# A new order of all engines for a two-layer gated mixture-of-experts block: the third batch's shared down products behind the experts, routing and puts batch by batch, the memsets of unused rows first

## The chip, the cores and the metric

One core of one Trainium2 chip. The metric is the device time of one run of the whole kernel in microseconds (us), given as the median of several runs.

## The reference

Input x has 4 batches of 256 tokens with 256 channels. Two layers are computed one after the other, `x = x + ffn(cond(x))`. The conditioning (bi_wkv) of both layers scans each channel over time forwards and backwards; k = v = the side input:

```python
ek = exp(min(k, 30)); ekv = ek * v
a = a * decay + ekv_t; b = b * decay + ek_t        # over t, forwards and backwards
num = nf + nb - ekv + exp(min(u + k, 30)) * v
den = df + db - ek + exp(min(u + k, 30))
out = sigmoid(r) * (num / max(den, 1e-8)) * (0.8 + 0.2 * tf)
```

Layer 0's ffn is a routed mixture with a shared part. Each token goes to its top 2 of 8 experts (capacity 320 rows each, places given out in the order of the tokens), each expert is `silu(gate) * up` of width 176 and a down product, weighted by a softmax of two logits. The shared part is the same with width 704 for every token. Layer 1's ffn is `relu(x @ W_up.T) @ W_down.T + sum(softmax(top 2 logits)) * (x @ W_expert)`.

## The kernel before

Engines are called PE (matrix products), DVE (vector), ACT (activations), POOL (GpSimd) and SP (DMA issue). Everything is held in SBUF; each engine runs one instruction stream written out in order, and semaphores tie the streams together. Tables of numbers at the head of the file say behind which "chunk" each engine does which piece of work.

A chunk is one hidden product. The shared part has 6 chunks per batch (5 of 128 hidden columns and one of 64), an expert has 2. The list `chunks` holds first the shared chunks of batches 0 to 2 and `SPLIT` chunks of batch 3 (together `nearly` = 20), then 16 of the experts (20 to 35), then the rest of batch 3. For a chunk PE makes the up and gate products (`shared_up`, `expert_up`; `hb` and at first `dn` are its PSUM banks), ACT takes the silu into `gate_a` (`silu`), DVE multiplies (`hidden`, into `hid` or `hidm`). PE may write a bank again only when the hidden product of the chunk that last used it is done (`chunk_before`). `shared_down(b)` is the down product of batch b's shared part, 12 matmuls into `dn`; `take_shared(b)` on DVE adds it to xt. `idle_products` are matmuls without use, `FILL` says how many stand ahead of which chunk.

The conditioning of a batch is cut in 6 steps (`wkv`): step 0 the forward scans of df, step 1 those of nf (and a cap of ek), step 2 and 3 the backward scans of df and nf (and a cap of euk), step 4 a reciprocal, step 5 the scaling of it. POOL does the products and sums between (`values`, `bonus`, `denominator`, `numerator`, `gate_num`, `hidden0`); for the batches in `H0_ON_VECTOR` DVE does the product h0 that ends them (`xc<-euv,rden`), for layer 1 those in `Q1_ON_VECTOR` the product `euk<-euv,rden`. `STEPS0` and `STEPS1` say how many steps of layer 0 and of layer 1 stand ahead of the hidden product of each chunk; ACT's scalings (`scale_fwd`) follow the same plan. `HOLD` names the numerators that POOL holds until DVE's step 4 has read.

Routing goes in rounds over batches (`ROUNDS`). `turn_rows(b)` on PE turns h0 to rows of tokens and makes the logits, ahead of the chunks in `TURN_AT`; ACT copies them (`turned`); `route(r)` on DVE picks the experts ahead of the hidden product in `ROUTE_AT`; `ranks(r)` on PE counts places behind the chunk in `RANK_AT`; `place(r)` on DVE makes `put_at` behind the hidden product in `PLACE_AT`. POOL then puts token rows with indirect DMAs (`scatter`, two for each of 8 tiles of tokens) into `slots_in` in DRAM; `SPREAD` says how many tiles have been put by which place of its stream. When all have landed SP loads them in pairs of experts (`load_pair`), PE turns them (`slots_T`, `tp<-ident,buf`), and they are split in two parts (`bufT`), as the experts' weights are (`mup_w`).

The experts' outputs go to `slots_out` in DRAM. Behind them POOL gathers them for each batch (`gather`), DVE adds them up to x1 (`combine`), PE turns x1 (`turn_x1`, `tp<-ident,xt`) and makes layer 1's products. Gathers start when the last expert's output is written and POOL has done what stands ahead of them, a numerator of layer 1 among it (`numerator`). The last batch's shared down product is split: its first tile stands ahead of `turn_x1(0)`, the second behind it.

Six memsets (`pads`) zero the unused rows of hid, sdn_s, hidm and mdn_s.

## Time and profile before

| | us |
|---|---|
| median of 3 runs (lowest, highest) | 180.54 (179.97, 181.22) |
| the profiled execution, span from first to last instruction | 168.4 |
| busy: PE, DVE, POOL, ACT | 151.0, 129.0, 102.4, 82.7 |

The profile records the profiled execution from its first to its last instruction; what lies ahead of it and behind it is in the run's time only. Its times count from the start of the span. Busy times overlap between engines, so their sum says nothing; what matters is which engine the chain of waits goes through. "xN" behind a PE row of a chain counts weight loads and matmuls together.

### The profile page before, as it was taken

What the parts mean: (1) busy time and instruction counts of PE and PEld (TensorE: products, weight loads), DVE (VectorE), ACT (ScalarE), POOL (GpSimd) and SP (SyncE); (2) the same over time, 40 slices, a digit from 0 to 9 for tenths busy, and PEclk for the clock granted to TensorE, in tenths of its full rate; (3) what the DMA queues carried; (4) which work ended last, traced back from release to release, by engine and by line L of the source; (5) the groups of instructions that cost most, each with busy time, mean ns of one, the idle gap of its engine ahead of it and who ended that gap; (6) DMA issues with size and microseconds to landing.
All of it is one profiled execution on the core that took longest, in us unless ns stands there. A gap on an engine that the chain in (4) does not pass through costs nothing.

```text
span 168.4 us, 2521 instructions
## 1 busy us (share of the span) xinstructions
PE 151.0 (90%) x790; PEld 133.2 (79%) x790; DVE 129.0 (77%) x290; ACT 82.7 (49%) x189; POOL 102.4 (61%) x109
## 2 busy tenths in 40 slices
PE   0398999999999999967999999999999929989991
PEld 0277888988898898854999999999988718879890
DVE  1899999979995987916467897899787845498634
ACT  3799951792372082103277853982734101336750
POOL 5376569796489877895049456637715777750330
PEclk9999999999999999995599999999999987999999
DMA  4789999996012132169402072022222333332211
GB/s 121 230 327 373 390 406 347 228 275 234 25 62 66 45 111 91 56 188 352 138 4 80 0 225 91 2 78 78 78 79 81 90 97 93 108 103 71 66 62 62
DMA packets 14844, 23.63 MB, mean 140 GB/s; under 512 B 1974, under 2 KB 10375, under 8 KB 14704
## 3 DMA queue, kind: packets, MB, share of 16 engines
q1 hardware_dynamic: 13152, 19.48, 35.8%
q0 software_dynamic: 1536, 3.99, 7.5%
q8 instruction: 6, 0.10, 0.3%
q14 instruction: 6, 0.05, 0.1%
q10 hardware_dynamic: 144, 0.00, 0.0%
HBM read 15.29 MB, written 8.39 MB: 141 GB/s over the span
## 4 chain that ended last, share of the span: by engine, by line
PE 72%; DVE 11%; DMA 6%; issue 5%; POOL 2%; ACT 2%; SPq 0%; DVEq 0%; POOLq 0%; ACTq 0%
PE hb L1057 31%; PE dn L1057 23%; PE tp L1057 5%; PE hb L1074 3%; PE tp L1178 3%; DMA buf<-slots_in 2%; PE dn L1074 2%; DMA wu_s<-wu 2%; POOL buf L512 2%; PE tp L1096 2%; DMA slots_in<-htok,put_at 1%; PE dk L1057 1%; DVE nf L777 1%; DVE xt L994 1%; DVE rden L859 1%
## 5 line engine op out<-in xcount | busy, mean ns | idle before, releaser
L1057 PE MATMUL hb<-xc,sup_s 128*128 128x256 f32 x136 | 30.8, 381 | 0.0
L1057 PEld LDWEIGHTS hb<-xc,sup_s 128*128 128x128 f32 x136 | 25.4, 190 | 3.2
L1057 PE MATMUL hb<-bufT,mup_w 128*112 128x320 f32 (+1 forms) x144 | 25.7, 336 | 0.7 <-issue 0.7
L619 ACT ACTIVATE gate_a<-hb 128x256 f32<-128x256 f32 (+3 forms) x38 | 15.1, 401 | 20.8 <-PE hb L1057 20.1
L1057 PEld LDWEIGHTS hb<-bufT,mup_w 128*112 128x112 f32 (+1 forms) x144 | 23.6, 195 | 1.5 <-issue 1.1
L1057 PE MATMUL dn<-sdn_s,hid 128*128 128x256 f32 x96 | 22.8, 394 | 0.1
L1057 PE MATMUL dn<-mdn_s,hidm 112*128 112x256 f32 x96 | 22.1, 380 | 0.0
L1057 PEld LDWEIGHTS dn<-sdn_s,hid 128*128 128x128 f32 x96 | 19.0, 200 | 3.2 <-DVE hid L887 0.5
L1057 PEld LDWEIGHTS dn<-mdn_s,hidm 112*128 112x128 f32 x96 | 17.7, 190 | 2.4 <-issue 0.3
L449 POOL TENSOR_TENSOR mup_w<-mup_s,mup_w 128x704 fp32r<-128x704 f32 x8 | 13.5, 1694 | 8.6 <-ACT mup_w L634 8.6
L422 POOL DMA_INDIRECT slots_in<-htok,put_at x16 | 15.9, 991 | 4.6 <-issue 4.3
L573 ACT ACTIVATE gd<-df,gain 128x255 f32<-128x255 f32 x16 | 8.1, 507 | 19.9 <-DVE df L770 19.5
L396 POOL TENSOR_TENSOR euk<-euk,df 128x512 f32<-128x512 f32 x7 | 8.9, 1278 | 7.8 <-DVE df L777 7.5
L403 POOL TENSOR_TENSOR euv<-euv,nf 128x512 f32<-128x512 f32 x7 | 9.0, 1279 | 7.3 <-DVE dk L819 4.9
L821 DVE RECIPROCAL dk<-dk 128x256 f32<-128x256 f32 x7 | 12.4, 1766 | 0.2
L887 DVE TENSOR_TENSOR hidm<-hb,gate_a 112x320 f32<-112x320 f32 (+1 forms) x16 | 7.6, 484 | 5.7 <-ACT gate_a L619 5.5
L1057 PE MATMUL dn<-k,ident 128*128 128x256 f32 x14 | 5.6, 585 | 7.0 <-DVE df L770 7.0
L380 POOL TENSOR_TENSOR euv<-euk,k 128x512 f32<-128x512 f32 x8 | 10.3, 1291 | 1.0 <-DVE euk L792 1.0
L777 DVE TENSOR_TENSOR_SCAN nf<-dk,nf,gn 128x255 f32<-128x255 f32 x14 | 9.6, 728 | 1.5 <-ACT gn L573 1.5
L1057 PEld LDWEIGHTS dn<-k,ident 128*128 128x128 f32 x14 | 4.2, 312 | 7.9 <-issue 6.9
L887 DVE TENSOR_TENSOR hid<-hb,gate_a 128x256 f32<-128x256 f32 (+1 forms) x22 | 9.1, 415 | 1.8 <-ACT gate_a L619 1.6
L895 DVE TENSOR_TENSOR bufT<-tp,bufT 128x512 fp32r<-128x512 f32 (+1 forms) x12 | 6.8, 594 | 4.7 <-ACT bufT L628 4.7
(146 smaller groups left out, 304.6 us busy)
## 6 DMA issues: line engine op xcount, KB each, us to landing
mup_s<-mup SPq DMA_DIRECT2D x4, 704.0 KB, 14.5
slots_in<-outb SPq DMA_DIRECT2D x10, 256.0 KB, 9.3
slots_out<-outb SPq DMA_DIRECT2D x8, 256.0 KB, 2.2
buf<-slots_in SPq DMA_DIRECT2D x4, 384.0 KB, 4.8
k<-k_cm SPq DMA_DIRECT2D x4, 256.0 KB, 4.8
xc<-x_cm SPq DMA_DIRECT2D x4, 256.0 KB, 8.0
sup_s<-sup SPq DMA_DIRECT2D x2, 512.0 KB, 8.7
xt<-x_tm SPq DMA_DIRECT2D x1, 1024.0 KB, 10.8
```

The source lines that it names most:

```text
L380: nc.gpsimd.tensor_tensor(euv[:, n % 2], euk[:, l, b], k[:, b], ALU.mult).then_inc(euv_ready, 1)
L396: nc.gpsimd.tensor_tensor(euk[:, l, b], euk[:, l, b], df[:], ALU.add).then_inc(den_summed, 1)
L403: nc.gpsimd.tensor_tensor(euv[:, n % 2], euv[:, n % 2], nf[:], ALU.add).then_inc(num_ready[n], 1)
L422: nc.gpsimd.indirect_dma_start(out=slots_in, out_offset=bass.IndirectOffsetOnAxis(ap=put_at[:, j, n:n + 1], axis=0), in_=htok[:, n], in_of ...
L449: nc.gpsimd.tensor_tensor(mup_w[:, e % 2, 1], mup_s[:, e], mup_w[:, e % 2, 0].bitcast(F32), ALU.subtract).then_inc(mup_low, 1)
L573: nc.scalar.activation(dst[:, c, 0:T - 1], fwd[:, c, 0:T - 1], ACT.Copy, scale=gain[:, l, b, c:c + 1]).then_inc(scaled, 1)
L619: nc.scalar.activation(dst, src, ACT.Silu).then_inc(silu_ready, 1)
L777: nc.vector.tensor_tensor_scan(rev(both[:, c, 0:T - 1]), d, rev(gained[:, c, 0:T - 1]), both[:, c, T - 1:T], ALU.mult, ALU.add).then_inc(b ...
L821: after(tick(nc.vector.reciprocal(pair, pair)))
L887: nc.vector.tensor_tensor(dst, up, g, ALU.mult).then_inc(hid_ready, 1)
L1057: return nc.tensor.matmul(dst, w, m, start=first, stop=last)
L1074: last = nc.tensor.matmul(ub[u][:, half * T:half * T + T], sup_s[:, at:at + P], xc[:, 0, c], start=c == 0 and half == 0, stop=c == CH - 1, ...
```

## The change

The first round of routing no longer takes two batches: there are four rounds, one for each batch. `SPLIT` is 4, so four chunks of batch 3 stand ahead of the experts (`nearly` = 22, experts 22 to 37) and two behind; `shared_down` has places ahead of the experts only for batches 0 and 1, and batch 2's stands behind the experts and behind the last shared chunks. The pads are zeroed ahead of `values(0)`. h0 of batch 2 moves from POOL to DVE, layer 1's q1 of batch 2 from DVE to POOL. All places of steps, routing, turns and fills are new. In all 12 idle products stand ahead of the shared chunks (12 and 7 before).

```diff
-ROUNDS = ((0, 2), (2, 3), (3, 4))
+ROUNDS = ((0, 1), (1, 2), (2, 3), (3, 4))
-SPLIT = 2
+SPLIT = 4
-FILL = {2: 5, 3: 7, 6: 7}
+FILL = {5: 9, 3: 2, 4: 1}
-HOLD = (1, 6)
+HOLD = (5,)
-TURN_AT = (6, 11, 15)
-ROUTE_AT = (6, 11, 15)
-RANK_AT = (7, 13, 16)
-PLACE_AT = (8, 12, 15)
+TURN_AT = (8, 13, 16)
+ROUTE_AT = (2, 8, 13, 16)
+RANK_AT = (5, 9, 15, 18)
+PLACE_AT = (5, 10, 14, 17)
...
-STEPS0 = (6, 1, 2, 0, 0, 0, 0, 0, 2, 4, 1, 0, 2, 0, 0, 0, 0, 0, 0)
+STEPS0 = (4, 2, 0, 0, 0, 2, 2, 0, 1, 1, 1, 1, 1, 1, 2, 0, 0, 0, 0, 0, 0, 0, 0, 0)
...
-DOWN_BEHIND = (10, 14, 19)
-TAKE_BEHIND = (15, 16, 19)
-GATE_AT = (6, 7)
-SPREAD = {5: 0, 8: 0, 10: 2, 11: 8, 13: 8, 14: 8, 15: 8}
-H0_ON_VECTOR = (0, 3)
-Q1_ON_VECTOR = (2, 3)
-PADS_AT = (5, 5, 5, 5, 5, 5)
+DOWN_BEHIND = (7, 15)
+TAKE_BEHIND = (11, 14)
+GATE_AT = (4, 7)
+SPREAD = {1: 2, 10: 4, 15: 8}
+H0_ON_VECTOR = (0, 2, 3)
+Q1_ON_VECTOR = (3,)
...
+            pool.wait_ge(consts, 7 + E)
+            for i, pad in enumerate(pads):
+                nc.gpsimd.memset(pad, 0.0).then_inc(padded, 1)
+                pool.wait_ge(padded, i + 1)
             values(0)
...
-                    pads_behind(4 * b + 1)
...
             halves()
+            for b in range(len(DOWN_BEHIND), B - 1):
+                take_shared(b)
             combine(0)
...
+                if b >= 1 and j == 0:
+                    pe.wait_ge(h0_ready[b], 1)
...
-                if b == B - 1:
+                if b == len(DOWN_BEHIND):
                     pe.wait_ge(mo_taken, 2 * E)
...
-                    pe.wait_ge(sh_taken, B - 1)
+                    pe.wait_ge(sh_taken, len(DOWN_BEHIND))
...
             for u in range(nlate, nchunks):
                 shared_up(u)
+            for b in range(len(DOWN_BEHIND), B - 1):
+                shared_down(b)
             shared_down(B - 1, range(TB - 1))
```

What stands in a row on POOL around the puts, before (`slots_in<-htok,put_at` is a put, `xc<-euv,rden` the product h0, `euv<-euk,k` the bonus, the three lines behind the first puts are denominator, numerator and gate of batch 3):

```order
L396 TENSOR_TENSOR euk<-euk,df 128x512
L403 TENSOR_TENSOR euv<-euv,nf 128x512
L408 TENSOR_TENSOR euv<-euv,xc 128x512
L413 TENSOR_TENSOR xc<-euv,rden 128x512
L380 TENSOR_TENSOR euv<-euk,k 128x512
L422 DMA slots_in<-htok,put_at 2560x256 x4
L396 TENSOR_TENSOR euk<-euk,df 128x512
L403 TENSOR_TENSOR euv<-euv,nf 128x512
L408 TENSOR_TENSOR euv<-euv,xc 128x512
L422 DMA slots_in<-htok,put_at 2560x256 x12
```

and now:

```order
L395 TENSOR_TENSOR euk<-euk,df 128x512
L402 TENSOR_TENSOR euv<-euv,nf 128x512
L407 TENSOR_TENSOR euv<-euv,xc 128x512
L379 TENSOR_TENSOR euv<-euk,k 128x512
L421 DMA slots_in<-htok,put_at 2560x256 x8
L395 TENSOR_TENSOR euk<-euk,df 128x512
L402 TENSOR_TENSOR euv<-euv,nf 128x512
L407 TENSOR_TENSOR euv<-euv,xc 128x512
L421 DMA slots_in<-htok,put_at 2560x256 x8
```

Batch 2's h0 has left the row, and eight puts (batches 0 and 1) stand ahead of batch 3's sums instead of four.

On DVE around experts 4 and 5, before (`hidm` 112x320 and 64x320 are the two hidden products of an expert, `bufT<-tp,bufT` the split of turned rows, `nf<-dk,nf,gn` the backward scan, the cap is `euk<-euk,dk`, step 4 are the three rows with `dk<-`):

```order
L887 TENSOR_TENSOR hidm<-hb,gate_a 64x320
L895 TENSOR_TENSOR bufT<-tp,bufT 128x2x256 x2
L887 TENSOR_TENSOR hidm<-hb,gate_a 112x320
L777 SCALAR_TENSOR_TENSOR nf<-dk,nf,gn 128x255 x2
L784 TENSOR_TENSOR euk<-euk,dk 128x512
L887 TENSOR_TENSOR hidm<-hb,gate_a 64x320
L895 TENSOR_TENSOR bufT<-tp,bufT 128x2x128
L818 TENSOR_TENSOR dk<-euk,dk 128x256
L819 SCALAR_TENSOR_TENSOR dk<-euk,dk 128x256
L821 RECIPROCAL dk<-dk 128x256
```

and now:

```order
L883 TENSOR_TENSOR hidm<-hb,gate_a 64x320
L891 TENSOR_TENSOR bufT<-tp,bufT 128x2x256 x2
L773 SCALAR_TENSOR_TENSOR nf<-dk,nf,gn 128x255 x2
L780 TENSOR_TENSOR euk<-euk,dk 128x512
L814 TENSOR_TENSOR dk<-euk,dk 128x256
L815 SCALAR_TENSOR_TENSOR dk<-euk,dk 128x256
L817 RECIPROCAL dk<-dk 128x256
L883 TENSOR_TENSOR hidm<-hb,gate_a 112x320
L883 TENSOR_TENSOR hidm<-hb,gate_a 64x320
```

The backward scan, the cap and all of step 4 have moved ahead of the first hidden product of expert 5.

On PE from the last experts' down products (`dn<-mdn_s,hidm`) to the second part of the last batch's down product, before:

```order
L1057 MATMUL dn<-mdn_s,hidm 128x256 x12
L1057 MATMUL hb<-xc,sup_s 128x256 x14
L1057 MATMUL dn<-sdn_s,hid 128x256 x6
L1238 MATMUL tp<-ident,xt 128x128 x4
L1057 MATMUL dn<-sdn_s,hid 128x256 x6
```

and now:

```order
L1055 MATMUL dn<-mdn_s,hidm 128x256 x12
L1055 MATMUL hb<-xc,sup_s 128x256 x6
L1055 MATMUL dn<-sdn_s,hid 128x256 x18
L1240 MATMUL tp<-ident,xt 128x128 x4
L1055 MATMUL dn<-sdn_s,hid 128x256 x6
```

Eight up products have gone ahead of the experts, and twelve down products have come.

## Rows read from the trace of the kernel before

**Rows 1.** The page, part 4: shares of the chain that ended last.

```profile
PE 72%; DVE 11%; DMA 6%; issue 5%; POOL 2%; ACT 2%; SPq 0%; DVEq 0%; POOLq 0%; ACTq 0%
```

**Rows 2.** Windows: busy us (and count) of each engine during the experts.

```profile
core 0: us, PE busy (x) PEld busy (x) DVE busy (x) ACT busy (x) POOL busy (x), PEclk, DMA share, GB/s
79.00:121.00 42.00, 42.00 (x247) 39.99 (x247) 34.44 (x56) 25.65 (x52) 22.62 (x16) 0.95 0.27 85
```

**Rows 3.** The chain in order of time (start, us, what), last put to first expert.

```profile
70.08 2.30 DMA slots_in<-htok,put_at
...
72.82 3.51 DMA buf<-slots_in
...
78.75 4.98 PE hb L1057 x18
```

**Rows 4.** Timeline, first values and the pads (start, us, engine line operation).

```profile
6.18 1.26 POOL L368 TENSOR_TENSOR ekv<-ek,k 128x512 f32<-128x512 f32 x1 [3.02 <-DVE ek L788]
...
7.90 1.26 DVE L770 TENSOR_TENSOR_SCAN nf<-dk,ekv 128x256 f32<-128x256 f32 x2
...
32.85 0.52 POOL L444 MEMSET hid<- 64x512 f32 x1
...
36.45 0.47 POOL L444 MEMSET hidm<- 64x128 f32 x2
```

**Rows 5.** Timeline of DVE: steps 0, 4 and the end of step 5.

```profile
18.31 1.27 DVE L770 TENSOR_TENSOR_SCAN df<-dk,ek 128x256 f32<-128x256 f32 x2
...
24.39 0.42 DVE L818 TENSOR_TENSOR dk<-euk,dk 128x256 f32<-128x256 f32 x1
...
27.72 0.42 DVE L887 TENSOR_TENSOR hid<-hb,gate_a 128x256 f32<-128x256 f32 x1
```

**Rows 6.** Timeline of DVE: one round of route, h0, and one round of place.

```profile
50.17 0.23 DVE L914 MAX8 top<-lg 128x8 f32<-128x8 f32 x2
...
51.16 0.41 DVE L887 TENSOR_TENSOR hid<-hb,gate_a 64x256 f32<-64x256 f32 x1
...
56.71 0.69 DVE L832 TENSOR_TENSOR xc<-euv,rden 128x512 f32<-128x512 f32 x1
...
57.78 0.18 DVE L932 TENSOR_TENSOR ohp<-tp,oh 128x32 f32<-128x32 f32 x1
...
58.57 1.27 DVE L770 TENSOR_TENSOR_SCAN df<-dk,ek 128x256 f32<-128x256 f32 x2
```

**Rows 7.** The chain in order of time: one batch's down products.

```profile
42.19 5.18 PE dn L1057 x24
```

**Rows 8.** The page, part 5: the puts (busy, mean ns, idle before).

```profile
L422 POOL DMA_INDIRECT slots_in<-htok,put_at x16 | 15.9, 991 | 4.6 <-issue 4.3
```

**Rows 9.** Line 837 (ns: shortest, median, longest): products of layer 1 on DVE.

```profile
L837 DVE TENSOR_TENSOR euk<-euv,rden x2: 692/1108/1524, 117.8 to 133.0; 128x512 f32<-128x512 f32 x2
```

**Rows 10.** Timeline of DVE around experts 4 and 5.

```profile
109.00 1.29 DVE L895 TENSOR_TENSOR bufT<-tp,bufT 128x512 fp32r<-128x512 f32 x2 [0.66 <-ACT bufT L628]
110.56 0.49 DVE L887 TENSOR_TENSOR hidm<-hb,gate_a 112x320 f32<-112x320 f32 x1 [0.27 <-ACT gate_a L619]
```

**Rows 11.** The chain in order of time: expert 6, last experts, last batch's down products.

```profile
113.12 2.63 PE hb L1057 x18
...
120.96 5.40 PE dn L1057 x24
...
139.40 3.68 PE dn L1057 x12
```

**Rows 12.** Timeline behind the experts: first gather, first transposes, second batch's sums.

```profile
130.08 1.02 POOL L512 DMA_INDIRECT buf<-slots_out,get_at  x1
...
138.31 1.09 PE L1238 MATMUL tp<-ident,xt 128*128 128x128 f32 x4 [3.00 <-DVE xt L999]
...
141.69 0.88 DVE L994 SCALAR_TENSOR_TENSOR xt<-buf,cw,xt 128x256 f32<-128x256 f32 x2 [0.85 <-DMA buf<-slots_out,get_at]
```

**Rows 13.** Windows: busy us and granted clock behind the first transposes of x1.

```profile
138.00:140.00 2.00, 1.69 (x6) 1.54 (x7) 0.56 (x2) 0.56 (x1) 1.57 (x2) 0.51 0.46 131
```

More of the change, by code:

```diff
@@ L31 @@
 L1X = CH * (2 * C + E)
-SPLIT = 2
+SPLIT = 4
 EARLY_AT = 1
 EARLY = 7
-FILL = {2: 5, 3: 7, 6: 7}
+FILL = {5: 9, 3: 2, 4: 1}
 AHEAD = 5
-HIGH_AT = (3, 10)
-HOLD = (1, 6)
-SILU_FIRST = (0, 1, 2, 3, 5, 7, 8, 13, 14, 16, 17, 18)
-TURN_AT = (6, 11, 15)
-ROUTE_AT = (6, 11, 15)
-RANK_AT = (7, 13, 16)
-PLACE_AT = (8, 12, 15)
-LOW_AT = (7, 8)
-FETCH_AT = 35
-STEPS = 6
-STEPS0 = (6, 1, 2, 0, 0, 0, 0, 0, 2, 4, 1, 0, 2, 0, 0, 0, 0, 0, 0)
-STEPS1 = (0, 0, 0, 0, 0, 0, 0, 0, 0, 0, 0, 0, 0, 1, 0, 1, 0, 0, 0, 2, 1, 0, 0, 0, 3, 2, 0, 2, 0, 3, 0, 1, 1, 0, 2, 0, 3, 1, 0, 1, 0, 0, 0, 0)
-DOWN_BEHIND = (10, 14, 19)
-TAKE_BEHIND = (15, 16, 19)
-GATE_AT = (6, 7)
-SPREAD = {5: 0, 8: 0, 10: 2, 11: 8, 13: 8, 14: 8, 15: 8}
-H0_ON_VECTOR = (0, 3)
-Q1_ON_VECTOR = (2, 3)
-PADS_AT = (5, 5, 5, 5, 5, 5)
+HIGH_AT = (4, 18)
+HOLD = (5,)
+SILU_FIRST = (0, 2, 5, 6, 7, 9, 10, 11, 13, 15, 17, 18, 20)
+TURN_AT = (8, 13, 16)
+ROUTE_AT = (2, 8, 13, 16)
+RANK_AT = (5, 9, 15, 18)
+PLACE_AT = (5, 10, 14, 17)
+LOW_AT = (8, 8)
+FETCH_AT = 33
+STEPS = 6
+STEPS0 = (4, 2, 0, 0, 0, 2, 2, 0, 1, 1, 1, 1, 1, 1, 2, 0, 0, 0, 0, 0, 0, 0, 0, 0)
+STEPS1 = (0, 0, 0, 0, 0, 0, 0, 0, 0, 0, 0, 0, 0, 0, 0, 0, 0, 1, 2, 0, 0, 1, 1, 0, 0, 1, 2, 2, 1, 0, 4, 0, 2, 0, 1, 3, 1, 0, 1, 1, 0, 0, 0, 0)
+DOWN_BEHIND = (7, 15)
[4 more added lines that the diff above has]
+Q1_ON_VECTOR = (3,)
 def adaln_ffn(nc, x_cm, x_tm, k_cm, cond, wu, router, sup, sdn, mup, mdn, l1w, out):
@@ L439, in _ @@
             pads = (hid[JR:P, :, JC], sdn_s[JR:P, JC], hidm[IB:IA, :, 1], mdn_s[IB:IA, :, 1], hidm[0:IB, :, 1, CAP:], hidm[:, :, 0, CAP:])
-            def pads_behind(step):
-                for i, pad in enumerate(pads):
-                    if PADS_AT[i] == step:
-                        nc.gpsimd.memset(pad, 0.0).then_inc(padded, 1)
-                        pool.wait_ge(padded, i + 1)
             def low_mup(e):
```

## The prediction

> **What bounds the kernel now.** I read the chain that ended last, then the windows, then each engine in order of time. In the chain [rows 1] TensorE (PE) has 72% of the span, VectorE (DVE) 11%, DMA 6%. During the experts PE is never idle: 42.00 us busy in the 42 us from 79 to 121 [rows 2]. PE stops in only two places. Before the experts it waits for the puts (the indirect DMAs that write token rows into slots_in): the last starts at 70.08 and lands after 2.30, and the loads that follow take until 76.33 [rows 3]; PE had been through its shared products 2.6 us before that, with two short idle times. Behind the experts it waits for the first gathers: they start at 130.08 and the transposes of x1 at 138.31, with PE idle for 3.0 us before these [rows 12]. So what counts is when the last put starts, whether PE stays fed between 79 and 126.4 (end of the experts), and what happens until 138.3.
>
> The profiled execution is known by its span, 168.4; the median of the runs is 180.54. I take the 12.14 between them as what lies around a span and leave it fixed.
>
> **Pads first.** The six memsets run from 32.85 to 36.45 + 0.47 = 36.92, 4.07 us [rows 4]. Ahead of the first batch they begin when the constants end (3.16), so end near 7.3. The product ekv then ends at 7.3 + 0.05 + 1.26 = 8.6, where it ended at 7.44. The scan of nf that needs it began at 7.90 [rows 4] and will begin at 8.65: +0.75 us on DVE and on the start of PE. That is certain within 0.25.
>
> **Routing batch by batch, from there to the last put.** I walk DVE's queue of the new order, in order, with measured pitches. Steps 0 to 3 with both caps took 18.31 to 24.39, 6.08; steps 4 and 5 took 24.39 to 27.72, 3.33 [rows 5]; of these a pair of scans is 1.16 to 1.30, a cap 0.58, step 5 0.61 and so step 4 2.72. Routing of two tiles took 50.17 to 51.16, 0.99; placing them 57.78 to 58.57, 0.79; a hidden product is 0.35; h0 on DVE is 0.69 and a wait, 0.84 more than step 5 alone [rows 6]. On PE twelve products take 5.18, so 0.432 each [rows 7].
> - DVE starts the second batch at 18.31 + 0.75 = 19.07. Steps 0 to 3, hid, steps 4 and 5, hid: 29.2. Routing of batch 0: 30.2. Three hids with ACT's tanh between: 31.4. Steps 0 and 1 of batch 2, cap, hid: 34.6. Place 0: 35.4. Steps 2, 3, cap, two hids, step 4: 42.0. Route 1: 43.0. hid, step 5 with h0, hid, step 0, hid, place 1: 47.5.
> - POOL, freed of the pads and of h0 of batch 2, has the values of batch 3 done by about 42.1 and puts batch 0 from there; a put costs 0.991 and (4.6 / 16) 0.29 of idle time, 1.28 [rows 8]. Batch 1's four follow at 47.5 and end at 52.6. Three products of 1.3 end at 56.7.
> - DVE from 47.5: step 1, hid, taking batch 0's sums (0.6), step 2, hid, step 3, cap, route 2, hid, steps 4 and 5 with h0, hid, place 2: 59.8. Only then may batch 2's puts start, so POOL waits 3 us. Four puts end at 64.9.
> - PE at 59.5 is through batch 1's down products; the turn of batch 3 waits for place 2 (59.8); 0.93 for the turn, ten products at 0.432 (4.3) and 0.35 for the ranks: 65.4. Place 3 ends at 66.2. The last four puts start at 66.25 to 70.1.
>
> So the last put starts at 70.1 against 70.08: 0.0. The chain is no longer POOL's issue but DVE's queue and PE's ranks. An uncertainty of 1 us each way is what 14 hids of 0.33 or 0.42 and the ACT waits make; if DVE's queue ran free of them POOL could start batch 2's puts at 56.7, and the last put 4.3 earlier at 65.8.
>
> One of the new terms is h0 of batch 2 on DVE. Its row beside POOL's puts is 0.69 [rows 6]; but the same kind of product, L837, took 1.524 beside a POOL product and 0.692 a second time [rows 9]. The Trainium skill (GPSIMD Engine Reference, section 1, Specifications) says that POOL shares its SBUF interfaces with VectorE and that they contend where a DVE instruction has two inputs in SBUF; the 1.52 agrees. In the new order POOL issues puts at that moment, so I take 0.69; by the page's rule with a product beside it, place 1 and all behind it would be 0.83 later.
>
> **PE's cut.** Seven idle products go, 12 down products move behind the experts and 8 up products come ahead of them: (7 + 12 - 8) x 0.432 = 4.75 us less PE ahead of the experts, all of it work beside the puts' chain. PE would be done at about 70.8 instead of 73.8 and be idle for 4.5 us until the first transposes. Since the last put sets these, this is worth nothing.
> It touches the clock, though. After the two idle times before the experts the first expert's 18 products took 4.98 [rows 3] where a later expert's take 2.63 [rows 11]: PE at the lower of its two levels for most of it, 2.35 lost. I take the same loss and 0.2 more for the longer idle time, between -0.6 and +1.1.
>
> **Experts.** The change puts 18 steps of the second layer among the 16 expert chunks, where 15 stood, and takes one product of 1.52 (L837) off DVE. PE needs the hidden product of a chunk before it may write its bank again, one expert later. The tight place is chunk 32, the first of expert 5: two steps now stand ahead of its hidden product, the scan of nf with its cap and step 4: 1.27 + 0.58 + 2.72 = 4.57. In the trace DVE was free of bufT at 109.00 + 1.29 and did the hidden product of expert 5 at 110.56, after 0.27 of waiting for ACT [rows 10]. By the new order I find DVE free at 109.55 (the hidden products of expert 4 are done 0.8 earlier, and bufT follows ACT), so the hidden product ends at 109.55 + 4.57 + 0.45 = 114.55. PE reached expert 6 at 113.12 [rows 11]. PE stalls for 1.45. At chunk 28 (step 4 ahead of it) hid ends at 101.5 where PE wants it at 101.6: 0. At chunk 35 (three steps ahead) 121.6 against 121.55: 0.05. Sum +1.5; bounds 0 (DVE early by 1.5) and +3.0 (late by 0.5 at each of the three). So the experts end at 127.9 instead of 120.96 + 5.40 = 126.36 [rows 11].
>
> **Tail.** The gathers waited for nf's numerator of the last batch on POOL, which now stands among the experts. What is left is expert 7's store: issued 0.8 after the products end, landing 2.0 later. The first gather starts 3.0 behind the experts' end where it started 3.72 behind (130.08 [rows 12] - 126.36): -0.7. PE behind the experts: 6 + 12 + 6 products, 10.4 us, against 20 products, 8.6; the transposes come 11.25 behind, so PE's idle time shrinks from 3.0 to 0.9. The moved 5.18 us is thus half hidden in what was idle, at no cost to the end.
> After the 3.0 idle the clock was granted at 0.51, the lower level, from 138 to 140 [rows 13]; six down products took 3.68 [rows 11] where they take 2.59, and the four transposes about 0.6 too much: 1.7 lost. With 0.9 of idle I expect the full clock. Of this only part reaches the end: batch 1's gathers already end the wait of DVE at 141.69 [rows 12], and they begin 0.8 later (+1.5 - 0.7). Its x1 is then ready at 144.25, its transposes end at 144.75 against 145.1, ACT's tanh starts at 144.8 instead of 145.49. So -0.7 from there on, where the experts' end was +1.5: the tail gives back 2.2.
>
> **Sum.** 0.0 + 0.2 + 1.5 - 2.2 = -0.5: a span of 167.9, and 180.0.
>
> **Rivals.**
> 1. Experts starved (slower). If DVE comes to chunk 32 later by 0.5 or more, the stall is 2 us and likely draws the clock down, as the idle time of 3.0 did [rows 13]; a low stretch cost 1.7 to 2.35, 2.1 in the middle. Then 180.0 + 0.5 + 2.1 = 182.6. For it: PE has no slack there [rows 2] and 4.57 us stand in one row. Against: ACT's waits may be shorter. It decides from a stall of some 2 us. Chance 0.23.
> 2. No stall: DVE is 1.5 earlier at chunk 32. Then 180.0 - 1.5 = 178.5. For it: DVE waited for ACT twice, 0.66 and 0.27, just ahead of this place [rows 10]. Chance 0.14.
> 3. Puts earlier. If place 2 is early enough that POOL never waits, the last put is up to 4.3 earlier, and PE, busy until 70.8, lets that through nearly whole; 2.5 as the middle: 177.5. Against: two DVE rounds are added to the queue and the pads cost 0.75. Chance 0.13.
>
> My forecast, in which puts, stall and tail nearly cancel, has 0.50.
>
> Below 1% a measurement of this kernel can hardly be told from no change. Faster by over 1% (under 178.7) are rivals 2 and 3: 0.27. Slower by over 1% (above 182.35) is rival 1: 0.23. The likeliest case alone spans 178.8 to 182.0; the range reaches to the middle of rival 3 and past rival 1: 177.4 to 183.0.
>
> **What would show it.** Right: POOL idle ahead of the ninth put, and the last put near 70; ekv ending at 8.6; PE idle for over 4 us before the experts; a stall of 1 to 2 us ahead of expert 6's products, released by hidm; the first gather 3 us behind the last expert product; a clock of 1.00 behind the transposes of x1. Wrong: no wait on hidm within the experts (rival 2), the last put before 68 (rival 3), a low clock among the experts (rival 1).

## The result, and the profile after

The changed kernel takes 187.96 us (median of 4 runs, 186.38 to 188.83) where the kernel before, run beside it, takes 180.88 (4 runs, 179.97 to 182.33): a ratio of 1.039, with the interval 1.030 to 1.047. It is slower by 7 us where 180.0 was forecast, outside the range. Here and below a ratio and its interval compare only the fast runs of the two kernels (some executions show a slower state), so they need not be the quotient of the medians beside them.

The profiled execution of the changed kernel has a span of 184.6 us and its own time is 186.38, so 1.8 us lie around a span, and not 12.14. The execution of before whose rows stand above (span 168.4) was some 10 us shorter than the runs beside which it stood. Why is told with the experiments; one of them gave a second trace of before, with a span of 179.0.

The chain that ended last, by engine [rows 1 before]:

```profile
span 184.6 us, 2510 instructions
...
PE 42%; DVE 29%; DMA 8%; issue 7%; another core or an unknown queue 6%; POOL 3%; ACT 2%; DVEq 0%; SPq 0%; POOLq 0%; ACTq 0%
```

PE had 72% of this chain and DVE 11%; now PE has 42% and DVE 29%. The chain now runs through DVE's queue for much of the time ahead of the experts. The part from the last put to the first expert, in order of time [rows 3 before]:

```profile
76.68 2.30 DMA slots_in<-htok,put_at
...
79.00 2.77 DMA buf<-slots_in
...
85.50 4.05 PE hb L1055 x18
```

The last put starts at 76.68 instead of 70.08, the first expert at 85.50 instead of 78.75. From the put on nothing has changed: 8.82 us between these two where there were 8.67. So the loss lies ahead of the last put. POOL's timeline shows what the puts wait for, and [rows 8] have their line of the page:

```profile
65.39 1.01 POOL L421 DMA_INDIRECT slots_in<-htok,put_at  x1 [6.44 <-DVE put_at L934]
...
72.85 0.97 POOL L421 DMA_INDIRECT slots_in<-htok,put_at  x1 [2.62 <-DVE put_at L934]
```

```profile
L421 POOL DMA_INDIRECT slots_in<-htok,put_at x16 | 15.8, 988 | 13.9 <-DVE put_at L934 9.1
```

A put is as cheap as it was (988 ns), but POOL stands idle for 6.44 us ahead of the ninth and for 2.62 ahead of the thirteenth, until DVE's put_at is written. So why is DVE late? The end of its third routing, in its timeline (a whole round took 0.99 us in [rows 6]):

```profile
55.48 0.16 DVE L913 FIND_INDEX8 idx<-top,lg 128x8 uint32<-128x8 f32 x1
55.56 2.08 DVE L914 TENSOR_TENSOR dtop<-top 128x2 f32<-128x2 f32 x1
57.56 0.18 DVE L918 TENSOR_TENSOR oh<-idx,iota_e 128x32 f32<-128x32 uint32 x1
57.77 1.21 DVE L919 TENSOR_TENSOR hot<-oh 128x16 bf16<-128x16 f32 x1
```

and POOL at the same time:

```profile
55.10 1.29 POOL L395 TENSOR_TENSOR euk<-euk,df 128x512 f32<-128x512 f32 x1
56.33 1.28 POOL L402 TENSOR_TENSOR euv<-euv,nf 128x512 f32<-128x512 f32 x1
57.68 1.26 POOL L407 TENSOR_TENSOR euv<-euv,xc 128x512 f32<-128x512 f32 x1
```

dtop subtracts two columns from two and takes 0.14 us in all three rounds of before. Here it lasts 2.08 us, and it ends at 57.64, when POOL's second product ends (57.61). hot, 0.17 otherwise, lasts 1.21 and ends at 58.98, when the third product ends (58.94). The first routing has the same (0.63 and 1.12), and slot of the first place (0.69 for 0.16). Behind it PE waits, since the counts of the round need hot, and its queue is in order:

```profile
59.03 0.18 PE L1055 MATMUL tp<-hot,before 128*128 128x16 bf16 x1 [3.03 <-DVE hot L919]
```

The tail, first in the chain [rows 11, 12 before], then as a window in which the seventh number is the granted clock [rows 13 before]:

```profile
127.53 5.39 PE dn L1055 x24
...
133.74 4.11 DMA slots_out<-outb
...
138.73 1.01 POOL buf L508
...
146.90 1.10 PE tp L1240 x4
...
148.61 11.39 another core or an unknown queue
...
160.09 0.70 ACT hid L709
```

```profile
146.00:153.00 7.00, 6.10 (x17) 5.01 (x18) 3.63 (x9) 0.60 (x1) 5.18 (x6) 0.51 0.33 94
```

The first gather starts 5.8 us behind the end of the experts (132.92), since the last small store of expert 7 took 4.11 to land (137.85) and the gather starts 0.88 behind that. The clock behind the transposes of x1 is again at its lower level (0.51). And 11.4 us of the chain end in ScalarE (ACT), released by nothing that the profile shows; the same wait is in the kernel before on such a chip (9.1 us in before_again below), so it is not the change's.

### The profile page after: what moved, and what is told of

Read it like the earlier page. It is cut to its first block, busy times and chain, and to the rows that moved or that the text cites. A ratio compares the mean times of both kernels' runs of the same rounds, so it can differ in the third digit from the quotient of the medians.

```text
span 184.6 us, 2510 instructions
## 1 busy us (share of the span) xinstructions
PE 153.5 (83%) x778; PEld 132.6 (72%) x778; DVE 134.4 (73%) x298; ACT 82.3 (45%) x190; POOL 102.0 (55%) x109
## 4 chain that ended last, share of the span: by engine, by line
PE 42%; DVE 29%; DMA 8%; issue 7%; another core or an unknown queue 6%; POOL 3%; ACT 2%; DVEq 0%; SPq 0%; POOLq 0%; ACTq 0%
PE hb L1055 19%; PE dn L1055 17%; DVE df L773 3%; DVE nf L766 3%; PE tp L1178 3%; DMA slots_out<-outb 2%; DVE df L766 2%; DVE nf L773 2%; DVE dk L817 2%; DVE hid L883 2%; DMA wu_s<-wu 2%; POOL buf L508 2%; DMA buf<-slots_in 1%; DMA buf<-slots_out,get_at 1%
## 5 line engine op out<-in xcount | busy, mean ns | idle before, releaser
L1055 PE MATMUL hb<-bufT,mup_w 128*112 128x320 f32 (+1 forms) x144 | 24.7, 327 | 0.7 <-issue 0.5
L1055 PEld LDWEIGHTS hb<-bufT,mup_w 128*112 128x112 f32 (+1 forms) x144 | 22.5, 188 | 2.2 <-POOL mup_w L442 1.0
L1055 PE MATMUL dn<-sdn_s,hid 128*128 128x256 f32 x96 | 24.0, 412 | 0.0
L1055 PEld LDWEIGHTS dn<-sdn_s,hid 128*128 128x128 f32 x96 | 19.8, 208 | 3.0
L508 POOL DMA_INDIRECT buf<-slots_out,get_at x8 | 7.6, 954 | 9.5 <-DMA slots_out<-outb 7.4
L1055 PE MATMUL dn<-htok,hid 128*128 128x256 f32 x32 | 9.5, 450 | 3.9 <-ACT hid L709 3.9
L395 POOL TENSOR_TENSOR euk<-euk,df 128x512 f32<-128x512 f32 x7 | 8.9, 1276 | 6.5 <-DVE df L773 6.3
L516 POOL TENSOR_TENSOR xt<-gate_a,xt 128x256 f32<-128x256 f32 x4 | 3.1, 797 | 16.7 <-ACT gate_a L728 16.7
L1178 PE MATMUL tp<-ident,buf 128*128 128x128 f32 x40 | 7.2, 313 | 5.2 <-DMA buf<-slots_in 4.9
L402 POOL TENSOR_TENSOR euv<-euv,nf 128x512 f32<-128x512 f32 x7 | 8.9, 1274 | 4.2 <-DVE dk L815 3.0
```

The costliest lines, as they stand in the source:

```text
L395: nc.gpsimd.tensor_tensor(euk[:, l, b], euk[:, l, b], df[:], ALU.add).then_inc(den_summed, 1)
L402: nc.gpsimd.tensor_tensor(euv[:, n % 2], euv[:, n % 2], nf[:], ALU.add).then_inc(num_ready[n], 1)
L508: nc.gpsimd.indirect_dma_start(out=got_of(b, j, i), out_offset=None, in_=slots_out, in_offset=bass.IndirectOffsetOnAxis(ap=get_at[:, j, b ...
L1055: return nc.tensor.matmul(dst, w, m, start=first, stop=last)
L1178: last = nc.tensor.transpose(tp[t % 2][:, at:at + P], buf[:, q % 2, 2 * i + k_, c * P:(c + 1) * P], ident[:])
```

## The experiments

Theory P: a small DVE operation lasts until the POOL product beside it ends, and the new order puts routings beside such products. Its rival, theory O: the order itself is late (four rounds for three, a batch's down products ahead of the last routing, counts two chunks behind it). The chips differ, as will be seen, so each time stands with that of before on the same chip.

### Parts of the change by themselves

The kernel before again, unchanged.

> The kernel before, unchanged, for a second trace. The first trace of it has a span of 168.4 where its runs take 180.9; the changed kernel's run of 186.4 has a span of 184.6, 1.8 around it. If 1.8 lies around every span, an ordinary execution of before has a span of about 179 and a stall of some 10 us that the first trace did not have: then ACT's wait behind the first x1 (5 us beyond its releaser in the changed kernel) should be seen here too. If instead 12 us lie around the span of before, this span is 168 to 170.

181.27 us. Its trace has a span of 179.0 where the one above had 168.4. The rows in which the two differ are ACT's; they follow below under the stall.

The fills first, alone, in the kernel before:

```diff
+            pool.wait_ge(consts, 7 + E)
+            for i, pad in enumerate(pads):
+                nc.gpsimd.memset(pad, 0.0).then_inc(padded, 1)
+                pool.wait_ge(padded, i + 1)
             values(0)
...
-                    pads_behind(4 * b + 1)
```

> Before, with the six memsets ahead of the first values and nothing else. Queue theory: the first ekv ends at 8.6 instead of 7.44, DVE starts batch 1 0.75 later, POOL has 4.1 us less around 33; the last put within 1 us of before, time +0 to +0.8 us. Port theory (a DVE instruction with two inputs in SBUF, or a plain scalar one, is held while POOL runs one): oscale and the first cap of ek take over 1.2 us each where they took 0.16 and 0.69, as in the changed kernel, but their wait lies inside the 0.75, so the same time: +0 to +0.8.

182.1, 0.8 above the same kernel without it. (Their ratios to before are 1.011, 1.004 to 1.018, and 1.009, 1.001 to 1.016, so by the time alone the two can't be told apart.) Every milestone ahead of the puts is 0.75 to 0.8 later (dtop of the first round 36.26 for 35.48, put_at 44.11 for 43.33). The term of +0.75 was right for these.

Batch 2's down products behind the experts, alone: the order of before with SPLIT 4, DOWN_BEHIND (10, 14), TAKE_BEHIND (15, 16), FETCH_AT 37, and the steps of layer 1 behind the two chunks more.

> Before's order with one part of the change: batch 2's shared down product behind the experts, two up chunks of batch 3 ahead of them (SPLIT 4), all tables of before otherwise, shifted by the two chunks. Queue theory: PE ends its work ahead of the experts 1.7 us earlier (idle there 3.1 instead of 1.4 us), the last put is where it was, PE's idle time behind the experts shrinks from 3.0 to about 1.3 us, and the time stays within 1 us. Rival (the cut of cover is what costs): more low clock at the first expert and batch 2's take on DVE late for the first x1, +2 us or more.

179.32, ratio 0.997 (0.991 to 1.003). This part costs nothing and gains nothing that can be told.

The fills back in their old place, but in the changed kernel:

```diff
-            pool.wait_ge(consts, 7 + E)
-            for i, pad in enumerate(pads):
-                nc.gpsimd.memset(pad, 0.0).then_inc(padded, 1)
-                pool.wait_ge(padded, i + 1)
             values(0)
...
                     pool.wait_ge(ekv_ready, b + 3)
+                    if b == 1:
+                        for i, pad in enumerate(pads):
+                            nc.gpsimd.memset(pad, 0.0).then_inc(padded, 1)
+                            pool.wait_ge(padded, i + 1)
```

> The changed kernel with the six fills of unused rows back behind the products of batch 1. Theory: the first values come 0.75 to 0.85 us earlier, but the fills then stand beside the first routing or behind it; everything up to the last put moves by no more than that, time 186.5 to 187.5 (0.5 to 1.3 less than the changed kernel's 187.96). Rival (the fills ahead hold the whole core back by more than their 0.8 us, since oscale and the cap of ek lasted 1.31 and 1.24 beside one of them): over 2 us less.

193.09, ratio 1.068 (1.059 to 1.078): neither theory, and 5 us worse than the changed kernel. PE's timeline says why:

```profile
41.08 8.11 PE L1055 MATMUL dn<-sdn_s,hid 128*128 128x256 f32 x24 [6.12 <-issue]
```

The first down products need the rows filled, and in the new order they stand behind chunk 7, not 10. With the fills ending at 40.98, PE stands for 6.12 us and then needs 8.11 for what takes 5.3, at a granted clock of 0.66 from 41.1 to 49.1. So the fills first cost 0.75 in the old order, and in the new one are what makes it possible at all. I had priced them only by the queue they stand in, not by who waits for them.

### POOL's products beside the routing

The numerator of batch 3 behind DVE's pair product, so that it and the gate product leave the third routing:

```diff
-HOLD = (5,)
+HOLD = (1, 3, 5)
```

> The changed kernel with HOLD (1, 3, 5) instead of (5,): POOL's numerators of batches 1 and 3 of layer 0 wait until DVE's step 4 has read, so no POOL product runs beside the routing of rounds 0 and 2. Port theory: dtop and hot of round 2 take 0.15 and 0.17 instead of 2.08 and 1.21, those of round 0 the same instead of 0.63 and 1.12; the place of round 2 comes 3 us or more earlier, the last put starts near 73 instead of 76.7, time -3 us against the changed kernel. Queue theory (DVE's instructions were merely waiting for something of their own): same lengths as in the changed kernel, and the numerators' wait makes it 0 to 1 us slower.

184.62, ratio 1.018 (1.008 to 1.027) where the changed kernel had 1.039: 3 us given back, 1.8 of them at the first expert (83.73). DVE's row beside the one product that stayed (L395, 55.27 to 56.55):

```profile
55.72 0.86 DVE L914 TENSOR_TENSOR dtop<-top 128x2 f32<-128x2 f32 x1
56.51 0.18 DVE L918 TENSOR_TENSOR oh<-idx,iota_e 128x32 f32<-128x32 uint32 x1
56.72 0.18 DVE L919 TENSOR_TENSOR hot<-oh 128x16 bf16<-128x16 f32 x1
```

dtop fell from 2.08 to 0.86 and hot from 1.21 to 0.18, when the products that had lain beside them went. The first routing kept its collisions (0.79 and 1.12): the expectation that they would go too failed, and the last put came at 74.83 where 73 was expected.

The same, and h0 of batch 1 moved to DVE, to free the first routing too (H0_ON_VECTOR (0, 1, 2, 3)).

> The changed kernel with HOLD (1, 3, 5) and H0_ON_VECTOR (0, 1, 2, 3): no product of POOL but one denominator stands beside a routing any more. Theory (the routing's small VectorE operations last until the POOL product beside them ends): in the first routing dtop takes 0.15 and hot 0.17 instead of 0.79 and 1.12, the h0 of batch 1 costs VectorE 0.69 more, so the first expert starts 0.5 to 1.0 us ahead of the 83.73 of the kernel with HOLD (1, 3, 5) alone, and the time is 183.5 to 184.5. Rival (the rounds batch by batch are late for another reason, and what the products cost there is covered): first expert within 0.3 us of 83.73, time as that kernel, 184.6 or above.

185.61, ratio 1.027 (1.018 to 1.035). The first routing is clean (0.14 and 0.17; in the third dtop still takes 0.87 beside the one denominator), and yet the first expert starts at 85.04, 1.3 later than in hold_num: the expectation failed. DVE and POOL:

```profile
29.25 1.67 DVE L828 TENSOR_TENSOR xc<-euv,rden 128x512 f32<-128x512 f32 x1 [0.34 <-POOL euv L407]
```

```profile
29.10 1.27 POOL L379 TENSOR_TENSOR euv<-euk,k 128x512 f32<-128x512 f32 x1
```

The moved product takes 1.67, for 0.69 otherwise: it now lies beside a POOL product itself. A collision was moved, not removed.

The other way round, in the kernel before: its first four puts taken away from beside the second routing, so that POOL's products stand there (the entry 10: 2 of SPREAD removed).

> The kernel before with one entry of SPREAD taken out ({13: 8, 14: 8, 15: 8}), so that POOL's products of batch 3 stand where the first four puts stood, beside the second routing. Theory (POOL's product holds the small operations): dtop of that routing, 0.14 now, lasts 0.5 to 2.1 us and hot, 0.17 now, 0.2 to 1.3; the sixteen puts in one row end at 73 to 75 and the time is 1 to 3 us above the kernel before. Rival (the long dtop and hot of the changed kernel come from something else in it, such as the form of one batch a round): both stay at 0.14 and 0.17.

181.54 beside 181.6; ratio 1.011 (1.003 to 1.018). dtop and hot kept their 0.14 and 0.17, as the rival said, but the operation between them did not:

```profile
50.69 0.14 DVE L918 TENSOR_TENSOR dtop<-top 128x2 f32<-128x2 f32 x1
50.81 1.25 DVE L922 TENSOR_TENSOR oh<-idx,iota_e 128x32 f32<-128x32 uint32 x1
```

POOL's gate product ran from 50.74 to 52.01; oh ends at 52.06. So it happens in the old order too, once a product lies there, and which of the small operations is caught depends on the moment. The last put came 2.1 later than in before_again, but the time did not follow.

H0 of batch 2 back on POOL (H0_ON_VECTOR (0, 3)).

> The changed kernel with h0 of batch 2 back on POOL (H0_ON_VECTOR (0, 3)). Theory: VectorE gives 0.69 up at 62.7 but POOL's product of 1.27 then stands there and ohp, slot or put_at of the third place last until it ends, so put_at(2) comes at 64.0 to 65.2 instead of 64.44, and the time is within 1 us of 187.96. Rival (the h0 on VectorE was one of the costs): 1 to 3 us less.

182.14 beside 170.35, ratio 1.055 (1.048 to 1.063). POOL waits 3.28 us for rden with h0 at the head of its queue, the puts begin at 50.05 and not at 44.30, put_at of the third place stands at 66.74 and not at 64.44, and the first expert starts at 89.93, where the unchanged kernel on such a chip has 86.12. So by the traces moving this h0 to DVE, which I had weighed as a cost of up to 0.83, is right in the new order. The times leave it open: the ratio to before is no worse than the 1.065 of after_again below (the intervals overlap), though the median is 2.7 us longer.

How much these products cost was measured by making them short, in kernels that leave that part of the computation out. First batch 1's h0 and batch 2's products (one of five edits):

```diff
-                nc.gpsimd.tensor_tensor(euk[:, l, b], euk[:, l, b], df[:], ALU.add).then_inc(den_summed, 1)
+                m = 8 if n == 2 else T
+                nc.gpsimd.tensor_tensor(euk[:, l, b, :, 0:m], euk[:, l, b, :, 0:m], df[:, :, 0:m], ALU.add).then_inc(den_summed, 1)
```

> The changed kernel with five of POOL's products cut to 8 of 256 columns: batch 1's h0, and batch 2's bonus, denominator, numerator and gate product, those beside the first and third routing. It leaves that part of the computation out. Theory: dtop and hot of both routings take 0.14 and 0.17, PE no longer waits 1.46 and 3.03 for hot, the third place ends near 60 and not 64.6, the last put starts at 71.5 to 73.5 and not 76.7, the first expert at 80.5 to 82.5 and not 85.5; 2 to 4 us of the 6.75 stay, by the new order. Rival (the order alone is at fault): the first expert still starts at 84 or later.

178.28 beside 170.38, ratio 1.065 (1.050 to 1.080), so the time shows no gain; the trace does. I had mistaken the batch: those beside the third routing are batch 3's, and it kept its 2.08 and 1.20. In the first routing dtop and hot are 0.48 and 0.94 shorter, 1.42 in all, and all of it arrives: first expert 84.72, for 86.12 in the unchanged kernel beside it. Then batch 3's too (n in (2, 3)):

> As after_short, but batch 3's denominator, numerator and gate product, those beside the third routing, are cut to 8 of 256 columns too. It leaves that part of the computation out. Theory: dtop and hot of the third routing take 0.14 and 0.17 instead of 2.08 and 1.21, PE's wait of 3.03 for hot goes, and the last put starts 2.5 to 3.2 us ahead of after_short's 75.91, at 72.7 to 73.4; the first expert starts at 81.5 to 82.3. So of 6.75 us some 4.4 are the products', some 2.5 the order's. Rival (the order alone): less than 1 us gained over after_short's 84.72.

173.65 beside 169.18, ratio 1.037 (1.017 to 1.056).

```profile
71.66 2.33 DMA slots_in<-htok,put_at
...
80.59 4.48 PE hb L1060 x18
```

dtop takes 0.14 and hot 0.17, PE's wait for hot is gone, the last put starts at 71.66 and the first expert at 80.59, earlier than expected. So of the 7.37 us by which the unchanged kernel was late on such a chip (86.12 - 78.75), 5.53 go with POOL's products and 1.84 stay with the order, 0.75 of it the fills and up to 0.53 the slot of the first place, which still lasts 0.69 for 0.16 beside a product. Of the 5.53, 4.38 are the four rows themselves (0.48 and 0.94, 1.93 and 1.03); the other 1.15 isn't parted by any run. Shorter products also shorten POOL's own queue, and the clock has a share: after the 3.03 us idle the 24 down products took 7.11 in after_again, at a granted clock of 0.76, and without the idle time 5.43. But the first trace of the changed kernel has the same idle time, then 5.3 for them at 1.00, and its first expert starts only 0.62 earlier (85.50), so the clock was worth some 0.6 there.

```profile
59.20 7.11 PE L1055 MATMUL dn<-sdn_s,hid 128*128 128x256 f32 x24
```

The last step of the order, counts one chunk closer to the routing (RANK_AT (5, 9, 15, 17)):

> The changed kernel with RANK_AT (5, 9, 15, 17): PE counts the last batch's tokens after 6, not 10, products of the row between. Theory (the last place waits 1.18 for these counts and VectorE's put_at ends at 72.07): put_at ends 1.0 to 2.2 us earlier, the last put starts at 74.5 to 75.7, and the time falls by 1 to 2 us against the changed kernel on the same kind of chip (179.4 beside 170.4, or 188.0 beside 180.9). Rival: PE waits for hot instead and nothing is gained.

179.02 beside 169.18, ratio 1.069 (1.051 to 1.087); nothing gained. PE's counts come 1.75 earlier (69.64 for 71.39 in after_again), put_at only 0.57, the last put at 76.70 for 77.27: ahead of the place DVE has a pair of scans and two hidden products of its own, and it had waited only 0.45 for the counts. The expected 1.0 to 2.2 was too much, read off a wait of 1.18 in another execution.

Which DVE operations are hit can be read from all twenty traces together with the kernel. In 53 cases a product or sum on DVE with both inputs in SBUF (dtop, oh, hot, slot, h0, q1, and one combine) started while a product of POOL was running. 52 of them were held until a product of POOL ended: the small ones ended with it, the long ones behind it (h0 and q1, 0.69 alone, 0.55 behind it). The 53rd started only 0.15 ahead of the end and kept its length. In 1274 cases one input was in PSUM, and every one kept its own length to within 0.05 us. The hidden products are of this second kind (`hb` and `dn` are PSUM banks), and so are the steps of the conditioning, since the pair, the decays and the caps lie in a fourth bank, `dk`:

```python
hb = [bank(f"hb{i}") for i in range(3)] + [bank("dk")]
```

```profile
41.62 1.27 POOL L407 TENSOR_TENSOR euv<-euv,xc 128x512 f32<-128x512 f32 x1
41.77 0.43 DVE L815 SCALAR_TENSOR_TENSOR dk<-euk,dk 128x256 f32<-128x256 f32 x1
```

POOL's fills, which read no tensor, and its puts and gathers held none of the operations with both inputs in SBUF: dtop, oh and hot beside a fill took 0.14 to 0.23 in all 25 cases. Who starts first counts too: h0 of the first batch started at 18.61, 0.16 ahead of POOL's product, and took 0.41. What is left open is why dtop at 55.56 was held through a second product and dtop at 29.68 was not, though in both the next product started just ahead of the end of the first.

### The stall of ScalarE

In before_again and three more kernels of its chip ACT stands still where its inputs are ready. ACT's timeline in the tail:

```profile
141.34 0.60 ACT L697 ACTIVATE hid<-tp 128x512 f32<-128x512 f32 x1 [6.63 <-PE tp L1238]
151.08 0.69 ACT L713 ACTIVATE hid<-hb,oscale 128x512 f32<-128x512 f32 x1 [9.14 <-remote]
154.56 0.60 ACT L697 ACTIVATE hid<-tp 128x512 f32<-128x512 f32 x1 [2.80 <-remote]
```

The product for the relu (L713) ended at 146.5; it starts 4.6 later. ("Remote" is a releaser that the profile doesn't have.) The next tanh has its input and starts another 2.8 behind the relu. In the first trace of before the same rows are at 144.90 and 145.49, each at once. A third stall, 3.1 us, lies at 62.75 to 65.87. What the three have in common is POOL: it issues indirect DMAs in one long row. In this trace two of the stalls end about when the row ends (the eighth put of such a row ends at 65.93; the sixteenth gather at 152.08), and the second tanh follows 2.5 behind it. In other traces they do not: in down_behind the relu starts at 150.63, with two gathers of the row still to come, and in after_clean the relu and the tanh start at 153.80 and 156.56 inside a row that goes on until 158.5. Theory G: the row holds ACT up. One wait more tests it:

```diff
+            pool.wait_ge(hid1_ready, 1)
             gather(3)
```

> The kernel before with one wait more: POOL's last four gathers wait for the first relu of layer 2 (hid1 of batch 0) on ScalarE. Theory G (ScalarE stands still while POOL issues a long row of indirect DMAs, and goes on when the row ends; in the runs its second tanh starts 2.5 us behind the end of the 16th gather, and one stall of 3.1 us ends with the 12th put): the relu that started at 151.08, 4.6 us behind its product, now starts at the end of the 12th gather, 147 to 149, the second tanh right behind it, and the time falls by 2.5 to 5 us, to 176 to 178. Rival (the stall is ScalarE's own, for instance its instructions arriving late): the relu starts at 151 as it did, the last gathers come later still, and the time is the same or 1 to 2 us longer.

175.36 beside 181.6: ratio 0.969 (0.960 to 0.977), the largest gain of the study. ACT again, and POOL:

```profile
150.14 0.69 ACT L714 ACTIVATE hid<-hb,oscale 128x512 f32<-128x512 f32 x1 [7.16 <-remote]
150.73 0.59 ACT L698 ACTIVATE hid<-tp 128x512 f32<-128x512 f32 x1
```

```profile
147.20 0.95 POOL L512 DMA_INDIRECT mup_s<-slots_out,get_at  x1 [0.30 <-issue]
151.10 0.94 POOL L512 DMA_INDIRECT mup_s<-slots_out,get_at  x1 [2.95 <-ACT hid L714]
```

The second stall is gone. The relu's own wait fell from 4.55 to 2.09: its product ended at 148.06, so that it starts 2.0 behind the twelfth gather. It starts at 150.14 and not at 147 to 149, nearer to the 151 of the rival; what speaks against the rival is the time, which fell, and the tanh, which no longer waits. Eight gathers held instead of four:

> The kernel before with the last eight gathers, not four, behind the first relu of layer 2. Theory G: the relu no longer waits for the 12th gather; it starts at 146.5 to 148.5 instead of 150.14. But the third batch's gathers come late, and VectorE's combine of it, which stands ahead of the first results, waits 3 to 6 us; the time is 175 to 178. If the relu still starts at 150, the gathers 9 to 12 had no part in it.

175.17 beside 170.35, ratio 1.031 (1.024 to 1.038). This run fell on another chip, and there ACT never stood still (nor in before, to judge by its 170.35 us for 181). The relu starts at 142.55, right behind its product, so nothing about the stall is learnt, and DVE's wait of 3.45 for the late gathers is a plain loss. Two more on that chip: batch 2's down products behind the experts, and the changed kernel with HOLD (1, 3, 5), both with the last four gathers held.

> The kernel with batch 2's shared down products behind the experts (SPLIT 4) in the order of before otherwise, and the last four gathers behind the first relu of layer 2. Theory G: the tail's second stall goes here too, so 179.32 falls by 3 to 5.5, to 174 to 176, and is level with or up to 1.5 us under the kernel before with that wait (175.36). Rival (the wait only repairs the order of before, since PE's products behind the experts shift the gathers' place): less than 1.5 us gained.

> The changed kernel with HOLD (1, 3, 5) and the last four gathers behind the first relu of layer 2. Theory (two separate costs: what VectorE loses beside POOL's products ahead of the experts, and the stall of ScalarE in the tail, which both kernels have): the tail gains as in the kernel before, 184.62 falls to 179 to 181.5, still 4 to 6 us over 175.36, since the first expert starts at 83.7 and not at 81.3 and the last stores land late. Rival (the changed kernel lost in its tail): within 2 us of 175.36.

168.9, ratio 0.996 (0.990 to 1.002), and 176.71, ratio 1.034 (1.026 to 1.042). Neither expected time counts any more, since each was made for a chip with the stall. But hold_g3 shows that the changed kernel's loss doesn't hang on the stall: with no stall anywhere it is still 6.4 us behind, and its first expert starts at 82.95. The last runs went to a third chip and were made to compare the two kernels without the stall.

> The changed kernel unchanged, beside the kernel before on the same chip. Theory (the front costs 5 to 7 us wherever it runs, the tail is the same or 1 us worse): where the kernel before takes 170 (ScalarE does not stand still), this takes 176 to 179; where it takes 181, this takes 186 to 188. dtop, hot and slot last 0.63, 1.12, 0.69, 2.08 and 1.21 as they did, on either chip. Rival (the loss depends on the chip, as the stall does): a ratio under 1.02 on a chip without the stall.

179.41 beside 170.38 (7 runs); ratio 1.065 (1.038 to 1.092). The loss is there without the stall too, and by the medians 9.0 us instead of 7.1. It looks smaller on the chip with the stall because there the kernel before loses time ahead of the experts too, by the stall of 3.1 us at 62.75: its first expert starts at 81.25 in before_again for 78.75, while the changed kernel has no such stall there and starts at 85.50 and 86.12. So the changed kernel is 4.25 late there on the one kind of chip and 7.4 on the other. dtop, hot and slot last 0.62, 1.12, 0.69, 2.07 and 1.20.

> The kernel before_g3 again. On a chip where ScalarE stands still: ratio 0.965 to 0.975; on one without, the relu of batch 0 is never late and the last four gathers are off the path, so 0.995 to 1.005.

> The kernel down_g3 again, on another chip. On a chip where ScalarE stands still: ratio to before 0.96 to 0.975; on one without: 0.985 to 1.0.

167.45 and 169.03 beside 170.38; ratios 1.000 (0.989 to 1.012) and 1.013 (1.000 to 1.026).

So the kernel before with its last four gathers held was 3% faster where ACT stalls and as fast, within the interval, where it does not: the version to keep, over both kernels. Batch 2's down products behind the experts add nothing that was measured.

## Why the prediction was wrong

Measured beside predicted, as differences to the first trace of before, for the changed kernel on the chip with the stall (span 184.6) and, in brackets, on one without (after_again, span 175.4).

- **Fills first, +0.75.** Right: the scan of nf starts at 8.65. Left out was that PE's first down products wait for them, which only the moved products make matter.
- **Last put, 0.0.** Wrong, +6.6 (+7.2), and this is the step that failed. I walked DVE's queue with pitches of before: "Routing of two tiles took 50.17 to 51.16, 0.99". That pitch was taken where POOL issues puts. The walk is right up to the first operation with both inputs in SBUF beside a POOL product: the first routing begins at 29.13 (29.2 predicted). It then ends 1.4 late, the first place 2.2, the second 2.0, and behind the third routing the third place is 4.8 late (64.6, not 59.8) and the fourth 5.9 (72.1, not 66.2). The products beside the two routings account for 5.5 at the first expert, 4.4 of it in the four rows themselves. I had the row for this: L837 took 1.524 beside a POOL product [rows 9]. The Trainium skill's rule (GPSIMD Engine Reference, section 1, Specifications: POOL shares SBUF interfaces with VectorE, with contention where a DVE instruction has two inputs in SBUF) was weighed for one instruction, h0 of batch 2, which is not among the ones that were hit; dtop and hot have two such inputs too. The traces agree with the rule wherever POOL runs a product (52 of 53 held, and none of 1274 with an input in PSUM), and not where it runs a fill: there dtop took 0.14. So the step put at nothing, with the rule at hand, was the length of the routing's and the place's small operations beside POOL's products.
- **PE's cut, worth nothing.** Right: PE is idle for 4.91 us ahead of the first transposes (4.5 predicted).
- **Clock, +0.2.** The first expert's 18 products took 4.05 (5.10), where 4.98 + 0.2 was meant: -0.9 (+0.1), and the -0.9 lies outside my bounds of -0.6 and +1.1.
- **Experts, +1.5.** Mis-sized: without the first expert's 18 products, from there to the last down product, it is +0.75 in both traces. It isn't one stall. The hidden product of expert 5 did not hold PE; PE waited 0.16 for expert 6, and that for POOL's mup_w, and the rest lies in pieces of 0.1 to 0.3 in experts 4 to 7. Why DVE was early enough at the steps that I had found too tight was not looked into.
- **Tail, -2.2.** From the end of the experts to the end of the span: 51.7 against 50.8 in before_again, +0.9 (and 40.8 against the first trace's 42.0, -1.2). The gather starts 5.8 (3.7) behind the experts and not 3.0. The term of -0.7 was misread. The gather of before (130.08) did start 0.15 behind the numerator (129.93), but expert 7's last store had landed only at 129.13, and in all ten traces with the numerator out of the way the first gather starts 0.88 behind that landing. I had left this 0.88 out; with it, taking the numerator away is worth 0.07 and not 0.7. On top, the small store (64 KB) took 4.11 (1.96) to land; in eight of the ten traces of the changed kernel and its variants it took 3.5 to 4.1, in all ten of the old order 1.96. Why is open. PE's idle time ahead of the transposes is 3.63 (1.68) and not 0.9; behind it the clock is 0.51 (1.00), so only in the trace with the quick store does something come back.
- **The frame.** 12.14 us "around a span" was a wrong reading. Every other run has 1.8, and the trace was of an execution without the stall of ScalarE beside times with it. By differences it did no harm to the forecast (before 180.5), but I should have asked what 12 us around a span could be.

None of the rivals was this one. Rival 1 looked for starved experts, and rival 3 for earlier puts. The range had 1 us each way for DVE's queue, from hidden products and ACT's waits, and nothing for operations made longer by POOL. The sum is 6.6 + 0.15 - 0.2 + (the tail) 9.65: 16.2 over the first trace, of which 10.6 are before's own on such a chip, and 5.6 remain; without the stall 7.2 + 0.2 + 0.9 - 1.2 = 7.1, or the 7.0 between the spans (175.4 - 168.4).

## What to carry to other kernels

A pitch taken from a trace holds only for the neighbours it was taken with. Before instructions are moved, lay the other engine's queue beside them: a DVE operation with both inputs in SBUF beside a POOL product can cost a whole product, however small it is (0.14 became 2.08), while one with an input in PSUM kept its length in every trace here, and what a new order moves next to a routing or another short chain counts in full. Price an edit also by who waits for its semaphore, in the new order and not in the old. And a trace whose span is much shorter than the run's time is a trace of another condition: take a second one before building on it. And where two waits end close together, as the numerator and the store ahead of the first gather did, taking one away gains only the distance to the other (0.07 here, priced at 0.7).

## What the hardware showed that was not expected

- A DVE operation on 2 to 32 columns with both inputs in SBUF lasted 0.62 to 2.08 us beside POOL products of 1.27, ending within 0.1 us of a product's end; across two products in a row, 2.08. None of 1274 operations with an input in PSUM was held. A one input operation did so as well: oscale, 4 columns, 1.31 for 0.16 beside a POOL fill, with the cap of ek behind it ending at the same moment.

```profile
5.46 1.31 DVE L755 TENSOR_SCALAR oscale<-gate_t 128x4 f32<-128x4 f32 x1
5.52 1.24 DVE L784 TENSOR_TENSOR ek<-ek,dk 128x512 f32<-128x512 f32 x1
```

- ScalarE stood still for 1 to 6 us at a time during long rows of indirect DMAs of POOL in each kernel profiled on two of the chips, and in none on three others; the same kernel takes 181 us on the first and 170 on the others. Breaking the row up once gave 3% back on a chip with the stall. That supports a tie between the row and the stall, in one kernel on one chip, and does not prove it: the relu still stood 2.09 us, and other stalls ended in the middle of a row. Through what the one would hold the other up, and what differs between the chips, no run tried.
